# A graph convolution by 32-row ranges on column tiles, its sums stored at fixed places and gathered by node

## The reference, cut to what matters

```python
y0, y1 = x0 @ lin1_w0, einsum(x1, lin1_w1)             # per node, scaled by a node factor
h = silu(edge_scalars @ fc_w1);  w = h @ fc_w2         # per edge: 8 -> 64 -> 4*64
xg0, xg1 = y0[edge_src], y1[edge_src]                  # gather one row of 256 per edge
mid0 = w_a * xg0 * ea0                                 # 64
mid1 = w_b * einsum('euc,ec->eu', xg1, ea1) / sqrt(3)  # 64: sum over three components
mid2 = (w_c * xg0)[:, :, None] * ea1[:, None, :]       # 3*64
mid3 = (w_d * ea0)[:, :, None] * xg1                   # 3*64
agg = segment_sum(concat(mid0..mid3), edge_dst)        # per node, 8*64 numbers
x = layernorm(x + self_part + agg @ lin2)              # node stage
x = layernorm(x + gat(x, src, dst))                    # attention, layernorm, elu
```

## Time and profile before

| what | us |
|---|---|
| median of 3 runs (6037.24 to 6047.06) | 6044.54 |
| the profiled execution | 6056.68 |
| its span, first to last instruction | 6055.1 |
| convolution loop, first load to last add | 205.7 to 3035.7 |
| node stage | 3080 to 3440 |
| attention loop | 3458 to 5597 |

### The profile page before, as it was taken

The page is one execution under the profiler, slowest core; times in us unless marked ns, Lnnn a source line. Parts: engine busy times, 40 slices in busy tenths (PEclk is TensorE's granted clock), DMA queues, the critical chain, the costliest instruction groups (busy, mean ns, idle before and its releaser), DMA issues. The chain is left out here.

```text
span 6055.1 us, 95297 instructions
## 1 busy us (share of the span) xinstructions
PE 4860.1 (80%) x19596; PEld 3238.8 (53%) x19596; DVE 4278.1 (71%) x12826; ACT 1755.5 (29%) x3895; POOL 3744.5 (62%) x3523
## 2 busy tenths in 40 slices
PE   2699999899989999999949788898888888988000
PEld 2454545454545454554549666676666666766000
DVE  0588888888888888888824366666666666666565
ACT  1333333333333333333314311111111111111333
POOL 0477777777777777777600177777777777775111
PEclk7899999999999999999979888888888888888555
DMA  8333333333333333333435444444444444444221
GB/s 366 122 96 95 93 94 91 94 94 95 92 95 93 95 94 94 94 93 94 88 142 233 166 117 118 118 117 118 117 117 118 117 117 117 118 118 91 99 91 68
DMA packets 318140, 695.26 MB, mean 115 GB/s; under 512 B 153201, under 2 KB 169203, under 8 KB 313971
## 3 DMA queue, kind: packets, MB, share of 16 engines
q0 software_dynamic: 181440, 518.30, 32.9%
q1 hardware_dynamic: 136626, 176.15, 8.4%
HBM read 554.55 MB, written 139.60 MB: 115 GB/s over the span
## 5 line engine op out<-in xcount | busy, mean ns | idle before, releaser
L429 POOL DMA_INDIRECT conv_xg<-y_rows,conv_ids x1680 | 1950.4, 1161 | 919.3 <-issue 411.4
L491 PE MATMUL conv_a<-conv_mids,conv_sel 128*128 128x512 f32 x3360 | 1860.8, 637 | 256.4 <-ACT conv_mids L530 255.7
L1431 POOL DMA_INDIRECT ord_xg<-xpa_rows,ord_ids x1680 | 1592.5, 948 | 518.5 <-issue 400.2
L530 ACT ACTIVATE conv_mids<-conv_raw,conv_ea 128x256 f32<-128x256 f32 x1680 | 823.9, 506 | 1475.7 <-DVE conv_raw L595 1474.5
L463 PEld LDWEIGHTS conv_w<-conv_fc,conv_ht 128*128 128x128 f32 x3360 | 676.5, 201 | 865.5 <-issue 851.9
L1498 PE MATMUL ord_a<-ord_xg,ord_sel 128*128 128x264 f32 x3360 | 1075.7, 465 | 43.3 <-DVE ord_xg L1714 39.0
L463 PE MATMUL conv_w<-conv_fc,conv_ht 128*128 128x256 f32 x3360 | 1053.7, 397 | 1.1 <-ACT conv_ht L506 1.1
L491 PEld LDWEIGHTS conv_a<-conv_mids,conv_sel 128*128 128x128 f32 x3360 | 646.0, 201 | 442.2 <-DVE conv_mids L601 325.8
L1498 PEld LDWEIGHTS ord_a<-ord_xg,ord_sel 128*128 128x128 f32 x3360 | 715.3, 228 | 195.4 <-DVE ord_xg L1714 66.7
L591 DVE TENSOR_TENSOR conv_raw<-conv_w,conv_xg 128x128 f32<-128x128 f32 x1680 | 479.9, 286 | 168.3 <-PE conv_w L463 166.6
L601 DVE TENSOR_TENSOR conv_mids<-conv_raw,conv_ea 128x192 f32<-128x192 f32 x1680 | 586.2, 349 | 0.0
(11 more groups left out here) (162 smaller groups left out, 4687.4 us busy)
## 6 DMA issues: line engine op xcount, KB each, us to landing
sum_rows<-conv_agg_s POOLq DMA_DIRECT2D x120, 256.0 KB, 4.1
conv_xg<-y_rows,conv_ids POOLq DMA_INDIRECT x1680, 2.9
ord_xg<-xpa_rows,ord_ids POOLq DMA_INDIRECT x1680, 2.8
mid_rows<-sum_rows SPq DMA_DIRECT2D x14, 1792.0 KB, 7.3
sum_rows<-lin_zeros POOLq DMA_DIRECT2D x12, 2048.0 KB, 38.6
head_rows<-ord_agg_s SPq DMA_DIRECT2D x120, 132.0 KB
xpa_rows<-mid_proj SPq DMA_DIRECT2D x14, 924.0 KB, 3.7
end_rows<-head_rows SPq DMA_DIRECT2D x14, 924.0 KB, 6.1
```

The lines of the kernel that those rows point to most:

```text
L429: nc.gpsimd.indirect_dma_start(xg[:, b, k], None, y, bass.IndirectOffsetOnAxis(ids[:, b, k:k + 1], 0))\
L491: nc.tensor.matmul(psum_a[b][:], sel[:, b, k], mids[:, k % HALF].rearrange("p q f -> p (q f)"), start=(k == 0), stop=(k == TILES - 1)).the ...
L530: nc.scalar.activation(mids[:, s, 0:4], raw[:, s, 0:4], ACT.Copy, scale=ea[:, b, 4 * k:4 * k + 1]).then_inc(ad_done, 1)
L1431: nc.gpsimd.indirect_dma_start(xg[:, b, k], None, xpa, bass.IndirectOffsetOnAxis(ids[:, b, k:k + 1], 0))\
```

## The change

Edges are cut anew: 139 groups of 4 ranges of 3 tiles (384 edges), 1668 tiles in all; a range reaches over fewer than 32 nodes. The table of sums has a place fixed by the range's number: row `(128 g + 4 r + s)` for group g, node r of range s; what the last node of a range has gathered so far is handed on to the next range by one-row multiplies. The node stage gathers its rows by a computed index (`node_row`). The zeroing of tables, the rounds and their barriers are gone from this path (they remain in the other branch of an If on the reaches found in `constants`; over the given inputs the four numbers compared with 128 are 112, 111, 104 and 100, so the new path is taken). Attention runs 119 groups in place of 120. Loops start at aligned addresses (`addr_align`).

The edge attributes are put into the selector: per tile `sel` is 128 x 4 x 32, one block of 32 columns for each of the four attributes, and the four multiplies land on partitions 32m to 32m+31 of one PSUM bank.

```diff
+    eng.addr_align(256, max_nops=32)                      # in_pairs, in_turns
 # project_sources: VectorE, instead of the memset of zeros
+                for t in range(NODE_TILES):               # 98
+                    nc.vector.scalar_tensor_tensor(out=passed[:, t % 2], in0=c["sub_place_b"][:, 0],   # 556 wide
+                                                   scalar=node[:, t:t + 1], in1=c["sub_place_b"][:, 1],
+                                                   op0=ALU.is_le, op1=ALU.mult, accum_out=moved[:, t:t + 1])
 # convolve_in_order, TensorE
+                def hidden(g, b, i, q, first):            # twice a group, 384 columns each
+                def weigh(g, b, u, early):                # for a pair of tiles
+                    for h in range(2):
+                        part = slice(h * MUL, (h + 1) * MUL)
+                        mm = nc.tensor.matmul(psum_w[:, 2 * (u % 2) + h, 0:4 * MUL], ht[part, b, u], fc2[part], ...)
+                def add_up(g, b, i, k):                   # for each tile
+                    for m in (1, 2, 3, 0):
+                        w, of = (4 * MUL, x[:, 0:4]) if m == 0 else (2 * MUL, x[:, 3 + m::4 - m])
+                        mm = nc.tensor.matmul(a[ROWS * m:ROWS * (m + 1), 0:w], sel[:, b, k, m], of, start=(j == 0), ...)
+                def hand_on(g, b, i, s):                  # for each range of 3 tiles
+                    pe.wait_ge(copied, GROUP_SUBS * g + s)
+                    for m in (1, 2, 3, 0):
+                        w = 4 * MUL if m == 0 else 2 * MUL
+                        mm = nc.tensor.matmul(psum_a[s % 2][ROWS * m:ROWS * m + 1, 0:w], hand_col[:, b, s, m:m + 1],
+                                              agg_s[..., (s - 1) % GROUP_SUBS, 0:w], start=False, stop=True)
 # order on TensorE for pair u of 6: [hidden of g+1 at u = 1, 3], then for both tiles k of the pair:
+                                add_up(g, b, i, k)
+                                if k % RUN == RUN - 1: hand_on(g, b, i, k // RUN)
+                                if k == 2 * u: weigh(pair u + 2)
 # ScalarE: two silu a group, one copy_out (128x256) a range, and two stores a group
+                    act.dma_start(rows[:, 0:8 * MUL].rearrange("(r s) (m f) -> m (r s) f", s=GROUP_SUBS, m=4),
+                                  agg_s[:, b, :, 0:2 * MUL])
+                    act.dma_start(rows[:, 8 * MUL:], agg_s[0:ROWS, b, :, 2 * MUL:])
 # VectorE: select, once a tile; products, once a pair; place and place_hands (small), once a group
+                    nc.vector.scalar_tensor_tensor(
+                        out=sel[:, b, k], in0=ramp.unsqueeze(1).to_broadcast([P, 4, ROWS]), scalar=rel[:, b, k:k + 1],
+                        in1=ea[:, b, k].unsqueeze(2).to_broadcast([P, 4, ROWS]), op0=ALU.is_equal, op1=ALU.mult)
+                    nc.vector.tensor_tensor(mids[:, d:d + 2, 0::7], w[:, :, 0:2], xg[...0:MUL], ALU.mult)   # 256
+                    for h in range(2):
+                        nc.vector.tensor_tensor(mids[:, d + h, 1:7], w[:, h, 2:4], xg[..., MUL:], ALU.mult)  # 384
 # GpSimd: one gather a tile, a buffer of 3 groups; no add
+                            nc.gpsimd.indirect_dma_start(xg[:, b, k], None, y, IndirectOffsetOnAxis(ids[:, b, 0, k:k + 1], 0))
 # node stage: rows by index, five blocks instead of four, one PSUM buffer for the transposes
+                        nc.gpsimd.indirect_dma_start(rows[:, b, j], None, sums, IndirectOffsetOnAxis(c["node_row"][:, ...], 0))
+                            for q in range(chunks):       # 5
+                                mm = nc.tensor.transpose(psum_s[n % buffers][:, q], rows[:, b, j, q], c["ident"][:])
 # gnn
-        project_sources(nc, io, c, y, [sums, heads])
-        start_windows(nc, c, "start0")
-        convolve_edges(nc, io, c, y, sums)
-        end_convolution(nc, io, c, sums, x1, xpa, att)
-        start_windows(nc, c, "start1")
+        project_sources(nc, io, c, y)
+        with nc.If(fit < WINDOW):
+            convolve_in_order(nc, io, c, y, sub_sums)
+            end_convolution(nc, io, c, sub_sums, x1, xpa, att, 5)
+            start_windows(nc, c, "start0")
+            attend_in_order(nc, io, c, xpa, att, heads)
```

More of the change, by code:

```diff
@@ L73, in in_turns @@
 def in_turns(eng, steps, turn, body, peeled=1):
+    last = math.ceil(steps / turn) - 1
     for i in range(peeled):
         body(i)
-    with eng.Fori(peeled, steps // turn - 1) as i:
+    eng.addr_align(256, max_nops=32)
+    with eng.Fori(peeled, last) as i:
         body(i)
-    body(steps // turn - 1)
+    body(last)
 def is_pair(i, n):
@@ L136, in _ @@
                 sp.dma_start(c["factor"][:], io["node_factor"]).then_inc(loaded, 16)
[L137 to L141, removed]
+                for name in ("first_dst", "last_dst", "sub_first", "sub_last"):
+                    sp.dma_start(c[name][:], io[name].rearrange("(o n) -> o n", o=1)).then_inc(loaded, 16)
+                sp.wait_ge(loaded, 80)
             @block.gpsimd
@@ L226, in _ @@
+                dve.wait_ge(moves, NODE_TILES)
+                nc.vector.scalar_tensor_tensor(out=c["node_row"][:], in0=node[:], scalar=float(GROUP_SUBS),
+                                               in1=moved[:], op0=ALU.mult, op1=ALU.add).then_inc(moves, 1)
             @block.gpsimd
             def _(pool):
[L229 to L237, removed]
@@ L271, in _, with clear_tables @@
                 in_pairs(act, BATCHES, pair)
+def clear_tables(nc, tables):
+    with Phase(nc, "clear") as ph:
+        zeros = ph.sb("zeros", [P, 4096])
+        zeroed, cleared = ph.sem("zeroed"), ph.sem("cleared")
+        with nc.Block() as block:
+            @block.vector
+            def _(dve):
+                nc.vector.memset(zeros[:], 0.0).then_inc(zeroed, 1)
+            @block.gpsimd
+            def _(pool):
+                pool.wait_ge(zeroed, 1)
+                n = 0
+                for table in tables:
+                    rows = table.rearrange("(p r) f -> p (r f)", p=P)
+                    width = rows.shape[1]
+                    for at in range(0, width, 4096):
+                        size = min(4096, width - at)
+                        pool.dma_start(rows[:, at:at + size], zeros[:, 0:size]).then_inc(cleared, 16)
+                        n += 1
+                pool.wait_ge(cleared, 16 * n)
 def rounds(nc, c, body):
@@ L623, in end_convolution @@
+def end_convolution(nc, io, c, sums, x1, xpa, att, chunks):
+    loads = 3 if chunks == 4 else 2
     TURN = 2 * BATCH - 1
     PAIR = 2 * BATCH
-    with Phase(nc, "mid") as ph:
+    with Phase(nc, f"mid{chunks}") as ph:
         w_self = ph.sb("w_self", [P, 2, P])
@@ L646, in end_convolution @@
         proj_a = ph.sb("proj_a", [P, 2, BATCH, 2 * HEADS])
-        psum_s = [ph.ps(f"s{b}", [P, 4, P]) for b in range(2)]
+        buffers = 2 if chunks == 4 else 1
+        psum_s = [ph.ps(f"s{b}", [P, 8 // buffers, P]) for b in range(buffers)]
         psum_z = [ph.ps(f"z{b}", [P, 512]) for b in range(2)]
@@ L1511, in turn @@
                         g = TURN * i + b
+                        if not has(i, b, 0):
+                            break
                         more = has(i, b, 1)
```

502 lines of the change are left out of this document (454 added, 48 removed).

## The result

The changed kernel takes 5193.89 us (median of 4 runs, 5191.44 to 5195.73), the kernel before 6045.8 in the same comparison: a ratio of 0.859 (0.858 to 0.861). The text forecast 5360, with TensorE as the limit; the time is that of its rival A, the gathers' pace, worked out there as 5195. The profiled execution took 5193.08 us.

A forecast was written before the change was run, and what follows sets the result against it. Three coupled engines bound the old loop; TensorE would set the new pace. From 6056.7: loop -568, ends -31, start -72, -5 and +4, node stage +3, attention -17.5 give 5370, less 12 told as 5360; range 5180 to 5830.

The forecast's parts named there:

- rival A: Convolution loop at the gathers' pace, TensorE under 1.25 us a tile; loop 2088 + 10, total 5195 us; chance 0.27.
- likeliest case: Convolution loop paced by TensorE at 1.35 us a tile, 2252 us; total 5360, own range 5250 to 5560; chance 0.38.
- Gathers: Convolution loop on GpSimd: 1668 gathers at 1.25 us a tile, 2088 us, no longer stretched by operations on two SBUF operands.
- TensorE: Convolution loop: multiplies on strips overlap in part, 0.536 us a set of add_up; 1.25 to 1.44 a tile, 1.35 taken.
- cheapest count: TensorE in the convolution loop, multiplies on different strips side by side: 2.50 us a pair of tiles, 1.25 a tile.
- turn: TensorE's switch between add_up, weigh and hidden, 2.3 a pair: waiting 0.163 us each adds 0.19 a tile, or is free.
- B, the number of instructions: Convolution loop: 13 load-multiply pairs at 0.125 us, 1.62 a tile; total 5817; chance 0.22 with all between 1.46 and 1.70.
- C, no overlap: Convolution loop: f32 multiplies on strips follow one another, 1.97 us a tile, loop 3286 + 10; total 6393; chance 0.11.
- VectorE: Convolution loop: VectorE needs 0.94 us a tile at most, under both other engines.
- Clock: Convolution loop: terms at full clock, granted 0.94 before; at 0.94 TensorE's term would be 140 us more.
- Start: Before the convolution loop: table ready near 120 us saves 72, windows leaving the path 5; `constants` costs 4 more.
- Seams, node stage, attention: Skipped rounds at the ends save 31 us, one attention group less 17.5; node stage and attention's zeros cost 3 more.

The follow-up runs named there:

- the ramp's run: Changed kernel with the ramp that `select` compares against read from SBUF in place of PSUM: 5221.09 us, ratio 0.862.
- half the gathers: Changed kernel with one gather for each pair of tiles in the convolution, the second tile using the first's rows: 4976.64 us, ratio 0.821.
- the first four: Changed kernel with half the gathers, one strip, ramp in SBUF, or zeroing back, where the kernel before took 6728.56 us: 0.926, 1.228, 1.122, 1.133.

## Why the prediction was right in its range, and which step failed

The time fell within the range and the sign was right, but by rival A and not by the likeliest case. The prediction named two signs of being wrong, a loop not bound by TensorE and a tile outside 1.29 to 1.46 us, and both came true: the range held because it had been drawn to take in rival A.

*Gathers: right.* 1.2505 us a tile against 1.25; loop 2101 against the 2098 of rival A. That they would be short because their neighbours read PSUM was borne out, and the ramp's run sharpened it.

*TensorE: this step failed.* It read: "each starts in program order and the two records of one multiply follow each other on their strip", so that the starts of a set are staggered by 0.107 and it takes 0.536 us. The order of starts is otherwise: all four first records within 20 ns, then the four second ones. A set then costs what its widest strip costs, two records of 256 columns 0.215 apart, 0.43 us, and the three strips of 128 columns run beside it. A `hand_on`, which has the same columns, adds 2.06 - 1.63 = 0.43, not 0.536. Two sets take 1.00 us up to the next `weigh`, where the step gave 2 x 0.536 + 0.215 = 1.29. The pair without the hidden layer is 1.63 us, or 2.06 with a `hand_on`, where the count gave 1.93 and 2.47. `weigh` was sized well, 0.63 against 0.645. The hidden layer was not: it adds 0.98 each time, twice a group, where the count had 0.645. Under my "cheapest count" of 1.25 a tile lay the real 1.12 (half the gathers), and that count was the only thing set against rival A.

The prediction quoted the Trainium skill, "TensorEngine Tiling (Array Packing)", section "Tiling Modes", on a drain at a change of mode. The trace leaves little room for one: from the last start of a set to `weigh` are 0.309 us (2204.660 to 2204.969), from the last start of a `weigh` to the next set 0.305 (1500.811 to 1501.116), and the 256 columns of each of these records take 0.215. So a turn costs at most 0.09 us each way, less than the 0.163 that I had taken from the earlier trace rows. The two halves of a `weigh`'s records, with no change of mode between them, stand 0.314 apart as well, so whether even the 0.09 is the turn's is open. By the Trainium skill, "TensorE: Matmul & The Clock Gate", Part 3, I had an estimate of 0.45 us for a set, with the loop at the gathers' pace: the trace agrees, with 0.43 us a set, and 0.57 with what stands before the next `weigh`.

*B, the number of instructions.* Not here: 21676 / 1668 is 13 pairs of load and multiply a tile, as counted, and they run at 1.12 us a tile in the half-gathers run, 0.086 a pair where B had 0.125. Its kin decided only on the chip of the first four.

*C, no overlap.* Priced right (6407 against 6393) and false: that strips overlap was to be judged, and it had 0.11.

*VectorE: right.* 1530.91 / 1668 is 0.918 us a tile busy against "0.94 at most"; 498.9 of the 563.0 us that it waits ahead of the products are for rows.

*Clock.* Granted 0.98 in the loop, where it was 0.94.

*Start.* 81 us against 72 + 5 - 4 = 73. The last two stores of `y_rows` are issued at 106.1 and 109.2, 79.5 us earlier than before (185.6 and 188.7), and the next stage's first instruction is at 115.8 where the table was forecast for 120. Pairs of batches took 13.7 us in the mean and not 14.0, and the projection's first load was 1.5 us earlier (13.3 against 14.8) where 4 more had been allowed for `constants`. The 98 new VectorE operations end at 88 and stay hidden.

*Seams, node stage, attention.* -33 against -31; +2 against +3, with wider index rows at no cost; -24 against -17.5. With 8 and 6.5 us more at the start and in attention, and 2 more in the seam, the node stage and the end together, the stages other than the loop gave 135 and not 118. Attention's 6.5 lie behind its last gather: from that gather's start to the last store are 28.6 us, where they were 35.4. That rival A's 5195 met 5193.89 so closely is partly chance: those 17 us more went against the 12 us that it took off for the median (5193.08 is within 1 us of its own) and the 3 by which it had the loop too quick.

## What to carry to other kernels

Find the engine that a loop cannot undercut (here one gather of 128 rows every 1.25 us) and ask what keeps it from that pace; the rest is worth doing only down to it, and half of it removed tells how far below the next limit lies (here 0.13 us a tile). When one buffer more or less is tried, follow the smallest load of the chain, the indices, and when it may start. Before an engine's cost is called a cheapest case, name the assumption on the order of its records (here a set of strips cost its widest strip); a rival with nothing else against it deserves more weight.

## What the runs showed of the hardware that was not expected

- Two-record f32 multiplies on four column strips are interleaved: first records 7 ns apart. Sets of 128, 128, 128 and 256 columns cost 0.43 us each, two records of the widest strip, and 0.57 where `weigh` follows; on one strip 1.15 (2.29 for two).
- A gather is lengthened when it starts inside a VectorE operation on two SBUF operands, in most cases by the rest of that operation less 0.13 us: 194 of 395 inside a compare of 128 elements (the changed kernel's own, one operand in PSUM: 1 of 381). An operation that begins while the gather runs does nothing in the ramp's run: of 591 such gathers none takes over 1000 ns.
- A gather of 128 rows costs GpSimd 0.946 us at 1 KB a row and 0.945 at 2.5 KB (mean of the 98 of the node stage); the wide rows land later, 7.1 us after the issue in the median where attention's, of about 1 KB, have 2.8.
- On one chip of those used, TensorE's instruction stream fell behind in stretches: variants within 1.5% of the changed kernel elsewhere took 1.12 to 1.13 times the kernel before there, at a granted clock of 0.75 in place of 0.88. The changed kernel itself was not run on it, and why that chip differs is open.
